# Twelve rounded layer-0 steps with their lower halves on GpSimd, six of sixteen chunks scaled in PSUM

## Chip, cores and metric

The kernel runs on one core of a Trainium2 chip. The metric is the device time of one execution in microseconds (us), as the median of several runs. The engines are called TensorE (PE in the rows; PEld is its weight load), VectorE (DVE), ScalarE (ACT), GpSimd (POOL) and SyncE (SP, which only issues transfers here).

## What is computed

The input has 512 rows of 64 fields with 16 elements each. Three layers follow; each makes the products of all fields of its input with the 64 original fields, and mixes them with a weight matrix into 128 outputs. Each layer's output is summed over the 16 elements and the three sums are put side by side.

```python
x_vec = input
outs = []
for W, b in params:
    z = jnp.einsum('bhd,bfd->bhfd', x_vec, input)
    B, h, f, d = z.shape
    z = z.reshape(B, h * f, d)
    x_vec = jnp.einsum('oc,bcd->bod', W, z) + b[None, :, None]
    outs.append(x_vec.sum(axis=2))
return jnp.concatenate(outs, axis=1)
```

Shapes: `input` is 512x64x16, `W0` is 128x4096, `W1` and `W2` are 128x8192, the result is 512x384, all float32.

## The kernel before

**Tiling.** A tile is 8 input rows times 16 elements, 128 columns. Four tiles make a group of 512 columns, and there are 16 groups. `body(n, kind)` exists once on each engine and runs for group 0 ("first"), groups 1 to 14 ("inner") and group 15 ("last"). Within it the place `e` runs from 0 to 63: tile `j = e // 16`, chunk `c = e % 16`. All engines walk the same places, each in its own written order, and wait for one another by semaphores.

**Layer 1, the bulk.** At each place `chunk` (L1008) makes y = x1 times 512 columns of W1 in three matmuls (`by_parts`, L875). Weights and x1 are split into an upper part, rounded to float32r, and a lower part, the rest; the products are upper by upper, upper by lower, lower by upper. A chunk covers four fields, and its 128x512 result lies in one of four PSUM banks (`y0` to `y3`, bank `c % 4`). The result must be multiplied by the four fields of x0 (`x0t`, one scalar per partition and field) and added up over all fields. It goes one of three ways:

- direct (`add_fields`, L716): VectorE multiplies and adds the bank into `acc` with four instructions of 128x128 (L738, L740);
- scaled (`SCALED`): ScalarE multiplies the bank in place with four instructions (`scale`, L627), then VectorE adds all 512 columns to `acc` with one instruction (L725);
- helped (`HELPED`): ScalarE writes the products to `prod` in SBUF (`multiply`, L638), and GpSimd adds them to `pacc` (`add_products`, L443 and L445).

Of 16 chunks, five are helped (1, 4, 7, 10, 13), three scaled (3, 9, 15) and eight direct. `chunk` waits until the chunk four before it, which had the same bank, has been taken out. Around an add, VectorE waits for its own instructions: L725 waits until the direct chunk before it is finished, and the first direct instruction behind L725 waits until L725 is finished (`acc_step`).

GpSimd's `combine` (L447) adds `acc` and `pacc` of the tile before (L451), folds the four fields (L453, L456) and so makes `x2`, which `layer2` (L996) needs at chunk 12 of the following tile. `own_rows` (L690) makes the other operand of `layer2` on VectorE, once a tile.

**Layer 0, one group ahead.** Layer 0 of group n+1 is made during group n in 17 steps, at the places `AHEAD_AT` (9, 11, 14, 17, 20, 23, 26, 29, 32, 34, 37, 40, 43, 46, 49, 52, 55; in group 0 between 24 and 55, and group 0's own steps at places 3 to 13 with 384 columns). For each step SyncE brings a shifted copy of the fields into one of six slots of `z`, and GpSimd multiplies it by the fields (`product`, L435). A step in `WHOLE` is one float32 matmul (L901). A step in `PARTED` (1, 3, 5, 7, 9, 11, 13) is three float32r matmuls: ScalarE first rounds `z` to `zh` (`part_upper`, L503, six places ahead), and VectorE subtracts to get `zl` (`part_lower`, L679, four places ahead). Step 16 is a small rest (`left_parts`, `left_lower` at L687). A slot of `z` is given back to SyncE when `zl` is made, or for a whole step when TensorE has used it (`slot_free`, L342).

**Turn of the group.** At place 58 VectorE makes the lower part of three tiles of the next group's x1 (`lower`, L706, 128x384), at place 4 that of the last tile (128x128), and at place 6 it sums layer 0 (L713). In groups 4, 8 and 12 the third layer's matmuls for a quarter of the rows (L992) are put between places 18 and 25.

## Time and profile before

| | |
|---|---|
| median of 3 runs | 1110.55 us (1109.91 to 1111.24) |
| the profiled execution's own time | 1111.36 us |
| its span | 1109.6 us |
| granted TensorE clock, mean over the span | 0.991 |
| busy: TensorE, VectorE, ScalarE, GpSimd | 1078.9, 863.8, 713.5, 862.1 us |
| L740 on VectorE (direct) | 1792 instructions, 493.2 us busy |
| L725 on VectorE (adds of scaled chunks) | 192 instructions, 132.6 us busy |
| L679 on VectorE (lower parts) | 112 instructions, 104.8 us busy |
| L696 on VectorE (`own_rows`) | 64 instructions, 41.6 us busy |
| L445 and L443 on GpSimd (adding products) | 256 instructions, 343.3 us busy |
| L503 on ScalarE (rounding) | 112 instructions, 70.4 us busy |

The span runs from the first to the last instruction. Busy time of an engine is the union of its instructions; a TensorE matmul's end is modelled, since matmuls overlap, so the pace of TensorE is better read from the starts of like matmuls in the timeline. Idle time in a row is the time in which that engine had nothing running just before the instruction, with the releaser.

### The profile page before, as it was taken

The page shows a single profiled execution, that of the slowest core. Times are in us where ns is not written, and L with a number is a line of the kernel's source. Part 1 is how long each engine was busy: PE and PEld are TensorE (multiplying, and loading weights), DVE is VectorE, ACT ScalarE, POOL GpSimd, SP SyncE. Part 2 cuts the span into 40 slices and gives each one's busy share as a digit, 9 for nine tenths or more (in the row PEclk, how much of TensorE's full clock was granted, in tenths as well). Part 3 has the DMA queues.
Part 4 walks back from the last instruction along what each step waited for, and adds up shares of the span by engine and source line. Part 5 has one row for each costly group of instructions (what it writes and reads, how often), then busy time and mean ns, then how long its engine had stood idle before and what let it go on. Part 6 is the DMA issues. An engine that isn't in the chain of part 4 may idle for free.

```text
span 1109.6 us, 17740 instructions
## 1 busy us (share of the span) xinstructions
PE 1078.9 (97%) x4781; PEld 808.4 (73%) x4781; DVE 863.8 (78%) x2529; ACT 713.5 (64%) x2428; POOL 862.1 (78%) x727
## 2 busy tenths in 40 slices
PE   6889999999999999999999999999999999999997
PEld 5767677777778777777778777777777877777776
DVE  5665888889894788988885698888887588888981
ACT  2566767767673676767673676766766476676771
POOL 2457897989984799897976779797988579798560
PEclk8999999999999999999999999999999999999998
DMA  7743333223241332324332142333232232321000
GB/s 280 196 101 96 74 92 79 77 55 96 50 101 39 66 84 54 97 65 86 84 67 58 45 87 82 70 93 74 77 68 64 63 69 77 79 77 41 1 23 8
DMA packets 108325, 85.87 MB, mean 77 GB/s; under 512 B 71040, under 2 KB 73824, under 8 KB 108096
## 3 DMA queue, kind: packets, MB, share of 16 engines
q1 hardware_dynamic: 106832, 78.17, 28.5%
q10 hardware_dynamic: 1392, 6.55, 1.9%
q8 instruction: 38, 0.62, 0.2%
q14 instruction: 63, 0.52, 0.2%
HBM read 14.75 MB, written 0.79 MB: 14 GB/s over the span
## 4 chain that ended last, share of the span: by engine, by line
PE 85%; DVE 6%; ACT 5%; issue 2%; DMA 1%; POOL 1%; ACTq 0%; DVEq 0%
PE y L881 57%; PE l L901 11%; PE l L881 7%; PE xt L992 5%; PE l2p L1004 3%; DVE acc L740 3%; ACT prod L638 2%; ACT y L627 2%; DVE acc L725 1%; DMA gram<-in_L_rec_W_dram 1%; DVE gram L824 1%; PE l L951 1%; PE l2p L981 1%; ACT x1h L536 1%; DVE bd L696 0%
## 5 line engine op out<-in xcount | busy, mean ns | idle before, releaser
L740 DVE SCALAR_TENSOR_TENSOR acc<-y,x0t,acc 128x128 f32<-128x128 f32 x1792 | 493.2, 340 | 62.6 <-PE y L881 58.2
L638 ACT ACTIVATE prod<-y,x0t 128x128 f32<-128x128 f32 x1280 | 367.7, 380 | 221.7 <-PE y L881 215.3
L881 PE MATMUL y<-w1h,x1h 128*128 128x512 f32 x1024 | 469.1, 458 | 3.9 <-DVE acc L740 3.7
L881 PE MATMUL y<-w1h,x1l 128*128 128x512 f32 x1024 | 402.7, 393 | 0.0
L881 PE MATMUL y<-w1l,x1h 128*128 128x512 f32 x1024 | 401.8, 392 | 0.0
L435 POOL TENSOR_TENSOR z<-z,xg 128x512 f32<-128x512 f32 (+2 forms) x272 | 372.2, 1373 | 24.4 <-DMA z<-xg 24.4
L445 POOL TENSOR_TENSOR pacc<-pacc,prod 128x512 f32<-128x512 f32 x192 | 253.1, 1318 | 137.2 <-ACT prod L638 137.2
L881 PEld LDWEIGHTS y<-w1h,x1h 128*128 128x128 f32 x1024 | 193.5, 189 | 108.4 <-issue 40.6
L627 ACT ACTIVATE y<-y,x0t 128x128 f32<-128x128 f32 x768 | 215.2, 349 | 75.8 <-PE y L881 75.5
L881 PEld LDWEIGHTS y<-w1l,x1h 128*128 128x128 f32 x1024 | 193.2, 189 | 59.5 <-issue 29.0
L725 DVE TENSOR_TENSOR acc<-y,acc 128x512 f32<-128x512 f32 x192 | 132.6, 691 | 131.8 <-ACT y L627 129.6
L881 PEld LDWEIGHTS y<-w1h,x1l 128*128 128x128 f32 x1024 | 192.5, 188 | 42.9
L901 PE MATMUL l<-z,w0t 128*128 128x512 f32 (+1 forms) x288 | 144.8, 584 | 0.0
L443 POOL TENSOR_TENSOR pacc<-prod 128x512 f32<-128x512 f32 x64 | 90.2, 1410 | 43.9 <-ACT prod L638 43.9
L679 DVE TENSOR_TENSOR zl<-z,zh 128x512 fp32r<-128x512 f32 (+1 forms) x112 | 104.8, 935 | 0.8 <-ACT zh L503 0.8
L503 ACT CAST zh<-z 128x512 fp32r<-128x512 f32 (+1 forms) x112 | 70.4, 629 | 40.7 <-POOL z L435 40.3
L451 POOL TENSOR_TENSOR pacc<-pacc,acc 128x512 f32<-128x512 f32 x63 | 81.2, 1289 | 6.1 <-DVE acc L725 4.6
L992 PEld LDWEIGHTS xt<-gram,w2t 128*128 128x128 f32 x512 | 63.8, 199 | 3.2 <-ACT sums L543 1.2
L992 PE MATMUL xt<-gram,w2t 128*128 128x128 f32 x512 | 64.1, 283 | 0.8 <-ACT sums L543 0.8
L901 PEld LDWEIGHTS l<-z,w0t 128*128 128x128 f32 x288 | 53.8, 188 | 11.2
L738 DVE TENSOR_SCALAR acc<-y,x0t 128x128 f32<-128x128 f32 x192 | 54.9, 341 | 0.0
L453 POOL TENSOR_TENSOR pacc<-pacc 128x256 f32<-128x256 f32 x63 | 46.7, 742 | 4.9
(92 smaller groups left out, 652.6 us busy)
## 6 DMA issues: line engine op xcount, KB each, us to landing
z<-xg SPq DMA_DIRECT2D x480, 128.0 KB, 2.4
w2t<-in_L_rec_W_dram SPq DMA_DIRECT2D x8, 512.0 KB, 9.0
gram<-in_L_rec_W_dram ACTq DMA_DIRECT2D x8, 512.0 KB, 4.7
xg<-in_r_input_dram SPq DMA_DIRECT2D x30, 128.0 KB, 3.9
z<-xg SPq DMA_DIRECT2D x32, 96.0 KB, 2.7
z<-xg SPq DMA_DIRECT2D x15, 192.0 KB
gram<-in_L_rec_W_dram ACTq DMA_DIRECT2D x1, 2048.0 KB, 9.7
out_dram<-z SPq DMA_DIRECT2D x4, 192.0 KB, 1.9
```

The costliest lines, as they stand in the source:

```text
L435: nc.gpsimd.tensor_tensor(to[0:rows, :], to[0:rows, :], xg[0:rows, cols], ALU.mult).then_inc(z_made, 1)
L443: nc.gpsimd.tensor_tensor(pacc[:], prod[:, 0], prod[:, 1], ALU.add).then_inc(pool_step, 1)
L445: nc.gpsimd.tensor_tensor(pacc[:], pacc[:], prod[:, h % HSLOTS], ALU.add).then_inc(pool_step, 1)
L451: nc.gpsimd.tensor_tensor(pacc[:], pacc[:], acc[:, slot], ALU.add).then_inc(pool_step, 1)
L627: last = nc.scalar.activation(of, of, ACT.Copy, scale=x0t[:, j, f:f + 1])
L638: last = nc.scalar.activation(prod[:, h % HSLOTS, k, :], y[c % YB][:, k * O:(k + 1) * O], ACT.Copy, scale=x0t[:, j, f:f + 1])
L679: nc.vector.tensor_tensor(zl[:, i % ZHSLOTS, cols], zin(n, t), zh[:, i % ZHSLOTS, cols].bitcast(F32), ALU.subtract).then_inc(zl_made, 1)
L725: nc.vector.tensor_tensor(to, y[c % YB][:], to, ALU.add).then_inc(acc_step, 1)
L740: ins = nc.vector.scalar_tensor_tensor(out=to, in0=of, scalar=x0t[:, j, f:f + 1], in1=b1r[:] if m == 0 else to, op0=ALU.mult, op1=ALU.add)
L881: ins = nc.tensor.matmul(to, stationary, moving, start=(first and k == 0), stop=(last and k == 2))
L901: nc.tensor.matmul(l0[:, cols], w0t[:, WHOLE.index(t), :], zin(n, t), start=(t == 0), stop=False).then_inc(z_used, 1)
L992: last = nc.tensor.matmul(l2, w2t[:, f, :], gram[:, f, :], start=(f == 0), stop=(f == F - 1))
```

## The change

`PARTED` becomes all steps of the first 16 that aren't divisible by four: twelve rounded steps instead of seven, four whole instead of nine. `part_lower` moves from VectorE to GpSimd and gets three slots of `zl`; `zh` has three slots, shared with the rest step. `HELPED` shrinks to chunks 7 and 13, so that GpSimd adds once a tile; `SCALED` grows to 1, 3, 5, 9, 11, 15 (1, 3, 5, 9, 11, 12 in the last group); the eight others stay direct. `multiply` now waits for the whole of the tile before (`x2_made`), since `pacc` is gone and the sum is made in `prod`. `own_rows` moves to ScalarE as four instructions of 128x64. GpSimd's order is written by places: products eight places ahead (the first three of the group after next at 59, 61 and 63), lower parts four ahead, the combination of the tile before at chunk 4, the add at chunk 15.

```diff
-PARTED = tuple(range(1, 15, 2))
+PARTED = tuple(t for t in range(ZT - 1) if t % 4)
...
-ZHSLOTS = 2
+ROUNDED = PARTED + (ZT - 1,)
+RN = len(ROUNDED)
+ZHSLOTS = 3
+ZLSLOTS = 3
...
-HELPED = (1, 4, 7, 10, 13)
+HELPED = (7, 13)
 HN = len(HELPED)
 SUMMED = tuple(c for c in range(CHUNKS) if c not in HELPED)
-SCALED = (3, 9, 15)
-SCALED_LAST = (3, 9, 12)
+SCALED = (1, 3, 5, 9, 11, 15)
...
-HSLOTS = 3
...
 PARTED_AT = [{AHEAD_AT[t] - k: t for t in PARTED} for k in (6, 4)]
...
-PRODUCTS_AT = ((2, 1, 1, 1, 1), (1, 1, 1, 1, 1), (1, 1, 1, 1, 1), (1, 0, 0, 0, 0))
...
+PRODUCTS_AT = [AHEAD_AT[t] - 8 for t in range(ZT)]
+PRODUCTS_EARLY_AT = (59, 61, 63)
+ADD_AT = [c + 2 for c in HELPED]
+COMBINE_AT = 4
...
-        prod = sb("prod", [P, HSLOTS, CF, O])
-        pacc = sb("pacc", [P, CF, O])
+        prod = sb("prod", [P, HN, CF, O])
...
-                if h == 1:
-                    pool.wait_ge(x2_made, x2_ready(tile - 1))
-                    nc.gpsimd.tensor_tensor(pacc[:], prod[:, 0], prod[:, 1], ALU.add).then_inc(pool_step, 1)
-                else:
-                    nc.gpsimd.tensor_tensor(pacc[:], pacc[:], prod[:, h % HSLOTS], ALU.add).then_inc(pool_step, 1)
+                nc.gpsimd.tensor_tensor(prod[:, 0], prod[:, 0], prod[:, h], ALU.add).then_inc(pool_step, 1)
+
+            def part_lower(n, t):
+
+                i = PN * n + PARTED.index(t)
+                cols = LATER if n == 0 else slice(0, GROUP)
+                if i >= ZLSLOTS:
+                    before = i - ZLSLOTS
+                    pool.wait_ge(z_used, ZT * (before // PN) + PARTED[before % PN] + 1)
+                pool.wait_ge(zh_made, i + 1)
+                nc.gpsimd.tensor_tensor(zl[:, i % ZLSLOTS, cols], zin(n, t),
+                                        zh[:, zhslot(n, t), cols].bitcast(F32), ALU.subtract).then_inc(zl_made, 1)
...
+                part = prod[:, 0]
+                pool.wait_ge(prod_made, HN * tile + 2 * HN)
                 pool.wait_ge(acc_step, tile_added(tile))
                 pool.wait_ge(pool_step, pool_at(tile, HN - 1))
-                nc.gpsimd.tensor_tensor(pacc[:], pacc[:], acc[:, slot], ALU.add).then_inc(pool_step, 1)
...
+                        for t in range(ZT):
+                            if at[t] == e and (kind == "first" or t >= len(PRODUCTS_EARLY_AT)):
+                                product(n + 1, t)
+                        if e in lower_at[1]:
+                            part_lower(n + 1, lower_at[1][e])
+                    if c == COMBINE_AT and (kind != "first" or j > 0):
                         combine(tile - 1, (j - 1) % 2)
...
+                        if c == ADD_AT[h]:
+                            add_products(tile, h)
+                    if e in PRODUCTS_EARLY_AT and n + 2 < GROUPS:
+                        product(n + 2, PRODUCTS_EARLY_AT.index(e))
...
+            def slot_of_parts(n, t):
+
+                i = rounded(n, t)
+                if i >= ZHSLOTS:
+                    before = i - ZHSLOTS
+                    act.wait_ge(z_used, ZT * (before // RN) + ROUNDED[before % RN] + 1)
+                return i % ZHSLOTS
...
+                    if c == OWN_AT:
+                        own_rows(tile, j)
...
+            def own_rows(tile, j):
+
+                act.wait_ge(l2p_made, layer2_ready(tile - 2))
+                act.wait_ge(own_made, 1)
+                for b in range(HALF_B):
+                    last = nc.scalar.activation(bd[:, j % 2, b * F:(b + 1) * F], x0t[:, j, :], ACT.Copy,
+                                                scale=own_half[:, b:b + 1])
+                last.then_inc(bd_made, 1)
...
-                before = h - HSLOTS if h >= HSLOTS else max(range(h, HN, HSLOTS))
-                act.wait_ge(pool_step, pool_at(tile, max(before, 1) - (POOL_STEPS if h < HSLOTS else 0)))
+                act.wait_ge(x2_made, x2_ready(tile - 1))
...
-            def part_lower(n, t):
-
-                i = PN * n + PARTED.index(t)
-                cols = LATER if n == 0 else slice(0, GROUP)
-                dve.wait_ge(zh_made, i + 1)
-                nc.vector.tensor_tensor(zl[:, i % ZHSLOTS, cols], zin(n, t),
-                                        zh[:, i % ZHSLOTS, cols].bitcast(F32), ALU.subtract).then_inc(zl_made, 1)
...
-            def own_rows(tile, j):
-
-
-                dve.wait_ge(l2p_made, layer2_ready(tile - 2))
-                dve.wait_ge(own_made, 1)
-                shape = [P, HALF_B, F]
-                nc.vector.tensor_tensor(bd[:, j % 2, 0:GRAM].rearrange("p (b f) -> p b f", f=F),
-                                        x0t[:, j, :].unsqueeze(1).to_broadcast(shape),
-                                        own_half[:].unsqueeze(2).to_broadcast(shape), ALU.mult).then_inc(bd_made, 1)
...
-                    if c == OWN_AT:
-                        own_rows(n * TILES + j, j)
...
-                    if kind == "inner" and e in PARTED_AT[1]:
-                        part_lower(n + 1, PARTED_AT[1][e])
...
                     i = PARTED.index(t)
-                    at = (PN * n + i) % ZHSLOTS
                     pe.wait_ge(zl_made, PN * n + i + 1)
-                    by_parts(l0[:, cols], zh[:, at, cols], zl[:, at, cols], w0h[:, i, :], w0l[:, i, :],
-                             t == 0, False, False).then_inc(z_used, 1)
+                    by_parts(l0[:, cols], zh[:, zhslot(n, t), cols], zl[:, (PN * n + i) % ZLSLOTS, cols],
+                             w0h[:, i, :], w0l[:, i, :], t == 0, False, False).then_inc(z_used, 1)
```

On VectorE the order changes at every tile. The first rows are from an inner group, tile 0 from its first chunk (`y0`, b1r) to the add of chunk 9, before:

```order
L740 SCALAR_TENSOR_TENSOR acc<-y0,x0t,b1r 128x128
L738 TENSOR_SCALAR acc<-y0,x0t 128x128 x3
L740 SCALAR_TENSOR_TENSOR acc<-y2,x0t,acc 128x128 x4
L725 TENSOR_TENSOR acc<-y3,acc 128x512
L706 SCALAR_TENSOR_TENSOR x1l<-l0,b0c,x1h 128x128
L740 SCALAR_TENSOR_TENSOR acc<-y1,x0t,acc 128x128 x4
L713 TENSOR_REDUCE sums<-l0 128x32
L740 SCALAR_TENSOR_TENSOR acc<-y2,x0t,acc 128x128 x4
L679 TENSOR_TENSOR zl<-z,zh 128x512
L740 SCALAR_TENSOR_TENSOR acc<-y0,x0t,acc 128x128 x4
L725 TENSOR_TENSOR acc<-y1,acc 128x512
```

and the same stretch of the changed kernel, up to the add of chunk 9:

```order
L763 SCALAR_TENSOR_TENSOR acc<-y0,x0t,b1r 128x128
L761 TENSOR_SCALAR acc<-y0,x0t 128x128 x3
L748 TENSOR_TENSOR acc<-y1,acc 128x512
L763 SCALAR_TENSOR_TENSOR acc<-y2,x0t,acc 128x128 x4
L748 TENSOR_TENSOR acc<-y3,acc 128x512
L729 SCALAR_TENSOR_TENSOR x1l<-l0,b0c,x1h 128x128
L763 SCALAR_TENSOR_TENSOR acc<-y0,x0t,acc 128x128 x4
L748 TENSOR_TENSOR acc<-y1,acc 128x512
L736 TENSOR_REDUCE sums<-l0 128x32
L763 SCALAR_TENSOR_TENSOR acc<-y2,x0t,acc 128x128 x4
L763 SCALAR_TENSOR_TENSOR acc<-y0,x0t,acc 128x128 x4
L748 TENSOR_TENSOR acc<-y1,acc 128x512
```

The one L679 that stood here is gone, and where one L725 stood at chunk 3, there are now three, at chunks 1, 3 and 5, each between two direct chunks.

On GpSimd an inner group's stretch between two combinations (that of tile 0 and that of tile 1) reads before, with `pacc<-pacc,acc` the start of the second combination:

```order
L435 TENSOR_TENSOR z<-z,xg 128x512
L443 TENSOR_TENSOR pacc<-prod 128x512
L435 TENSOR_TENSOR z<-z,xg 128x512
L445 TENSOR_TENSOR pacc<-pacc,prod 128x512
L435 TENSOR_TENSOR z<-z,xg 128x512
L445 TENSOR_TENSOR pacc<-pacc,prod 128x512
L435 TENSOR_TENSOR z<-z,xg 128x512
L445 TENSOR_TENSOR pacc<-pacc,prod 128x512
L435 TENSOR_TENSOR z<-z,xg 128x512
L451 TENSOR_TENSOR pacc<-pacc,acc 128x512
```

and in the changed kernel, from the product at place 21 to the start of the second combination:

```order
L448 TENSOR_TENSOR z<-z,xg 128x512
L464 TENSOR_TENSOR zl<-z,zh 128x512
L448 TENSOR_TENSOR z<-z,xg 128x512
L464 TENSOR_TENSOR zl<-z,zh 128x512
L448 TENSOR_TENSOR z<-z,xg 128x512 x2
L464 TENSOR_TENSOR zl<-z,zh 128x512
L454 TENSOR_TENSOR prod<-prod 128x512
L448 TENSOR_TENSOR z<-z,xg 128x512
L464 TENSOR_TENSOR zl<-z,zh 128x512
L448 TENSOR_TENSOR z<-z,xg 128x512
L464 TENSOR_TENSOR zl<-z,zh 128x512
L473 TENSOR_TENSOR prod<-prod,acc 128x512
```

Three of four adds of products are gone from a tile, and lower parts (`zl`) stand between the products instead.

## Rows read from the trace of the kernel before

**Rows 1.** The profile's page, span and busy time of each engine

```profile
span 1109.6 us, 17740 instructions
...
PE 1078.9 (97%) x4781; PEld 808.4 (73%) x4781; DVE 863.8 (78%) x2529; ACT 713.5 (64%) x2428; POOL 862.1 (78%) x727
```

**Rows 2.** Windows: span, then busy us (records) of each engine

```profile
513.10:527.80 14.70, 14.66 (x59) 10.43 (x60) 13.94 (x41) 11.11 (x40) 14.54 (x13) 1.00 0.22 58
560.10:574.40 14.30, 14.12 (x59) 10.12 (x58) 11.37 (x36) 10.34 (x37) 8.87 (x9) 1.00 0.54 106
513.10:574.40 61.30, 61.08 (x252) 44.66 (x253) 52.44 (x156) 42.96 (x150) 54.61 (x46) 1.00 0.32 77
1032.50:1083.20 50.70, 49.68 (x217) 37.02 (x217) 46.12 (x146) 39.65 (x145) 30.25 (x28) 1.00 0.04 13
```

**Rows 3.** Timeline of TensorE, two layer-0 steps: start us, length us, instruction

```profile
587.21 0.39 PE L881 MATMUL y<-w1l,x1h 128*128 128x512 f32 x1
...
587.66 1.02 PE L901 MATMUL l<-z,w0t 128*128 128x512 f32 x2
...
588.75 0.39 PE L881 MATMUL y<-w1l,x1h 128*128 128x512 f32 x1
...
590.14 0.39 PE L881 MATMUL y<-w1l,x1h 128*128 128x512 f32 x1
...
591.51 0.39 PE L881 MATMUL y<-w1l,x1h 128*128 128x512 f32 x1
```

**Rows 4.** Timeline of TensorE, tile 3 chunk 8 to the next tile 0 chunk 10

```profile
567.96 0.40 PE L881 MATMUL y<-w1l,x1h 128*128 128x512 f32 x1
...
573.60 0.39 PE L881 MATMUL y<-w1l,x1h 128*128 128x512 f32 x1
...
574.41 0.47 PE L881 MATMUL y<-w1h,x1h 128*128 128x512 f32 x1 [0.19 <-DVE acc L740]
574.72 0.39 PE L881 MATMUL y<-w1l,x1h 128*128 128x512 f32 x1
...
582.72 0.39 PE L881 MATMUL y<-w1l,x1h 128*128 128x512 f32 x1
```

**Rows 5.** Timeline of VectorE: chunks 8 to 11; the end of a tile

```profile
522.17 1.11 DVE L740 SCALAR_TENSOR_TENSOR acc<-y,x0t,acc 128x128 f32<-128x128 f32 x4
523.39 0.69 DVE L725 TENSOR_TENSOR acc<-y,acc 128x512 f32<-128x512 f32 x1
524.18 1.12 DVE L740 SCALAR_TENSOR_TENSOR acc<-y,x0t,acc 128x128 f32<-128x128 f32 x4
...
575.60 0.69 DVE L725 TENSOR_TENSOR acc<-y,acc 128x512 f32<-128x512 f32 x1 [0.31 <-ACT y L627]
576.21 0.34 DVE L740 SCALAR_TENSOR_TENSOR acc<-y,x0t,b1r 128x128 f32<-128x128 f32 x1
```

**Rows 6.** Timeline of ScalarE, one chunk scaled in PSUM

```profile
528.12 1.11 ACT L627 ACTIVATE y<-y,x0t 128x128 f32<-128x128 f32 x4 [0.56 <-PE y L881]
```

**Rows 7.** Groups by line and shape: count, busy us, mean ns, idle

```profile
L679 DVE TENSOR_TENSOR zl<-z,zh 128x512 fp32r<-128x512 f32 x105 | 100.4, 956 | 0.8 <-ACT zh L503 0.8
...
L453 POOL TENSOR_TENSOR pacc<-pacc 128x256 f32<-128x256 f32 x63 | 46.7, 742 | 4.9
...
L456 POOL TENSOR_TENSOR x<-pacc 128x128 f32<-128x128 f32 x63 | 32.5, 516 | 4.9
...
L713 DVE TENSOR_REDUCE sums<-l 128x32 f32<-128x512 f32 x16 | 10.9, 680 | 0.0
L687 DVE TENSOR_TENSOR zleft<-z,zleft 32x512 fp32r<-32x512 f32 x15 | 10.3, 687 | 0.5
L706 DVE SCALAR_TENSOR_TENSOR x1l<-l,b0c,x1h 128x384 fp32r<-128x384 f32 x16 | 9.7, 607 | 0.0
...
L951 PE MATMUL l<-acc,w0t 128*128 128x128 f32 x6 | 1.0, 275 | 0.0
```

**Rows 8.** GpSimd line L435: shortest, median, longest ns

```profile
L435 POOL TENSOR_TENSOR z<-z,xg x272: 991/1291/1775, 22.4 to 1019.0; 128x512 f32<-128x512 f32 x120, 128x384 f32<-128x384 f32 x8, 96x512 f32<-96x512 f32 x7, 96x384 f32<-96x384 f32 x1
```

89 lines of the change are left out of this document (42 added, 47 removed).

## Prediction

> **What bounds the kernel now.** I read the page first: TensorE is busy for 1078.9 of 1109.6 us, VectorE and GpSimd for 78% each [rows 1]. An average hides which stretch has which limit, so I went to the windows of one inner group. Its 61.3 us are 14.7 in tile 0, 14.3 in tile 3 and so 32.3 in tiles 1 and 2; VectorE is busy for 52.4 us of the group, but for 13.94 of 14.70 in tile 0 [rows 2]. The reason is the schedule: no layer-0 step stands between places 56 and 8, so TensorE turns out chunks fastest just there. Then the timelines. The second matmul of a chunk starts at 588.75 and that of the chunk two later at 590.14, so a chunk alone costs 0.695 us; with a whole step between, the distance is 1.54, with a rounded one 1.37 [rows 3]. A whole step therefore costs 0.85 and a rounded one 0.68. The last of the views shows the first sign of the other limit: the last chunk of tile 3 comes 1.12 us behind its forerunner instead of 0.695, because VectorE (releaser L740) had not emptied the bank [rows 4]. TensorE is the bound, with VectorE close behind at the turn of the group.
>
> **What the rounded steps give.** Five steps a group go from 0.85 to 0.68: -0.85 us in each of the 15 groups made ahead, of which bodies 1 to 14 are the inner ones.
>
> **What VectorE loses and gets.** In each inner group it loses seven lower parts (0.96 us each in the mean [rows 7]) and four `own_rows`. It gets three more adds a tile, twelve a group. Their price is in the timeline [rows 5]. Four direct instructions take 1.11 us and each lasts 0.34, so they start 0.26 apart: 1.04 a chunk. The add starts 0.11 behind the end of the fourth (522.17 + 1.11 = 523.28, then 523.39), lasts 0.69, and the next chunk starts 0.10 behind its end (524.08, then 524.18). From the fourth direct instruction's start (522.94) to the next chunk's first it is 1.24 instead of 0.26: **an add between two direct chunks costs 0.98**, not 0.69. At a tile's end nothing waits behind the add (575.60 to 576.21 is 0.61), so it costs 0.11 + 0.08 + 0.61 = 0.80.
>
> A tile of VectorE before: 8 x 1.04 + 2 x 0.98 + 0.80 = 11.1. After, with five adds inside and one at the end: 8.3 + 4.9 + 0.8 = **14.0**. TensorE's chunks of a tile, without steps, take 16 x 0.695 = 11.1. In tiles 1 and 2 five or six steps a tile keep TensorE slower than VectorE. In tiles 3 and 0 they don't.
>
> **The turn of the group.** Take the stretch from the start of tile 3's chunk 8 to that of the next tile 0's chunk 10. Today it takes 14.76 (567.96 to 582.72), 0.43 of it the wait above [rows 4]; none of its steps changes its form. In the changed order it begins when VectorE has emptied chunk 4's bank and ends when it has emptied that of tile 0's chunk 6. Between these lie nine direct chunks (6, 8, 10, 12, 14, 0, 2, 4, 6), six adds inside (5, 9, 11, 1, 3, 5) and one at the tile's end (15): 9.36 + 5.88 + 0.80. Add the lower parts of x1 (0.607 less the overlap of 0.08, so 0.52; and 0.26 for the narrow one) and the sum (0.60) [rows 7]. These three fill the waits beside an add, 0.18 each, so -0.54. It makes 16.9, **+2.1 us** against 14.76.
>
> Before the stretch VectorE is late already. From the start of tile 2's last chunk TensorE needs nine chunks and the steps 14, 15 and 16 (0.68, 0.68, about 0.24) to reach chunk 8: 7.9. On the other side: the chunk (0.7), 0.2 to ScalarE, scaling 1.11 [rows 6], then on VectorE the add 0.61, chunk 0 1.04, add 0.98, chunk 2 1.04, add 0.80, the rest step's subtraction (0.687 [rows 7] and a gap, 0.72), chunk 4 1.12, and 0.2 to TensorE: 8.5. That is +0.6 to +0.8. About 0.2 more is a wait in tile 1, which VectorE enters three chunks behind. Sum of an inner group: -0.85 + 2.1 + 0.75 + 0.2 = **+2.2**, in 14 groups +31 us. A group then takes 63.5, though VectorE's work in it is only 4 x 14.0 + 2.1 = 58.
>
> **Last group.** No steps slow TensorE, so VectorE sets the pace throughout. With chunks 11 and 12 both scaled, a tile is 8.3 + 4 x 0.98 + 1.77 (two adds in a row: 0.19 + 0.69 + 0.10 + 0.69 + 0.10) = 14.0; four tiles, x1 and sum: 56.5 against 50.7 now [rows 2]. **+5.8.**
>
> **First group and start.** Five more steps have two weights instead of one in the early layer-0 matmuls: three of those (six records, two a float32 matmul) took 1.0 us [rows 7], so five take up to 1.7, on the path to the first chunk; from below, nothing, if something else is late there. I take +1.3. In group 0 the steps are 384 columns wide (5 x 0.13 saved) and tile 3 begins to suffer; GpSimd no longer stands waiting for products of chunks there. I take 0, with -2 and +4 as ends.
>
> **ScalarE.** Five more roundings, four x four `own_rows` instructions of 64 columns. These shapes aren't in the trace; from below, nothing, from above the 0.26 pace of 128 columns [rows 6], 1.04 a tile. With 5 x 0.55 that is at most 6.9 us on 43.0 busy of 61.3 [rows 2]: 49.9 of 63.5, hidden in its waits for TensorE. If the cover went, as much as 0.3 a tile in the last group: +1.
>
> **GpSimd.** Twelve adds of products go, twelve lower parts come. Its products of the same shape take 1.29 in the median, 1.775 at the longest [rows 8]; the lower part on GpSimd isn't in the trace. Between 0.99 and 1.775 I take 1.29, the nearest row: same shape, same kind, two inputs in SBUF. From the lower part of step 5 to that of step 14 it must issue 9 products, 7 lower parts, one add and two combinations (1.29 + 0.74 + 0.52 each [rows 7, 8]): 17 x 1.29 + 5.1 = 27.0 us, while TensorE walks the places 19 to 45 in 26 chunks, 3 whole and 6 rounded steps, 18.1 + 2.6 + 4.1 = 24.8, besides two layer-2 products and the transposes. So GpSimd works there almost without a pause, up to 2 us behind, against the four places (2.8 us and their steps) that a lower part is ahead: just covered. Behind a late lower part TensorE itself stands, behind a late combination ScalarE at chunk 7. SyncE gets twelve slots back from GpSimd; its transfers are issued in the same order, and a late early product at 59 holds up an add that is needed only at chunk 12 of the next tile.
>
> **Sum.** 31 + 5.8 + 1.3 + 0 = +38. Against the profiled execution's 1111.4 this is 1149.5; the median of the runs is 0.8 below that execution, so I predict **1148.5 us**.
>
> **Rivals.** *The waits around an add cost nothing* (4%). Then an add costs 0.61, the turn takes 9.36 + 7 x 0.61 + 1.38 = 15.0 and so +0.25, without the late entry: -0.6 a group, -8 in all; the last group is back at its 50 us; with the start 1103. For it: nothing in the rows; against it: both gaps are there at each such add [rows 5]. The Trainium skill says in "VectorE: DVE Perf Modes", section "The DRAIN you can't avoid", that the semaphore costs nothing extra. By that rule the time is this rival's; the trace disagrees, with instructions 0.26 apart where no wait is and 0.10 behind the end where one is.
>
> *GpSimd becomes the bound* (14%). If a lower part takes 1.6 instead of 1.29, the seven of the middle cost 2.2 more, some 1.7 of it behind its cover: +24, 1172 us. It decides from about 1.4. For it: products of up to 1.775; against it: the median of 1.29. The Trainium skill's "SBUF — State Buffer", section "Who interferes with whom", says that a VectorE instruction with two SBUF inputs contends with GpSimd's reads. By that rule the long products came from lower parts and `own_rows`, which go, and this rival loses weight; no row here shows GpSimd without them for a whole group.
>
> *TensorE stays the bound* (4%), with the four banks swallowing VectorE's lateness: only the rounded steps count, -13 - 0.6 + 1.3, 1098 us. Against it: the 0.43 lost today with three adds a tile fewer.
>
> *It cancels* (2%): gain and loss within 0.2%, which is about what a measurement of this kernel can tell from no change.
>
> **Numbers.** The forecast has 76%. Its own ends are a loss of 1.6 to 2.9 a group (22 to 41) with the rest as above: 1139 to 1162. Reaching into the GpSimd case the range is 1138 to 1170 and leaves out under 2 in 10. Faster 0.08, same 0.02, slower 0.90.
>
> **What would show it.** Right: tiles 3 and 0 of an inner group together at 31 to 32 (29.0 now), tiles 1 and 2 at about 32 as now; the bank waits of TensorE on L725's and L740's successors from place 56 to 10; VectorE with gaps of 0.1 around each add and hardly any other idle time there; the last group at 56.5. Wrong: GpSimd without idle time and TensorE waiting for `zl`; adds closer than 0.1 to their neighbours; tiles 3 and 0 unchanged.

## The result and the profile after

The changed kernel takes 1155.43 us in the median of four runs (1153.61 to 1156.08), the kernel before, run beside it, 1110.89 (1109.91 to 1112.77): ratio 1.0393, interval 1.0378 to 1.0409. It is 44.5 us slower. The profiled execution took 1155.74 us.

The page, span and busy time of each engine, which answers to [rows 1]:

```profile
span 1154.0 us, 18359 instructions
...
PE 1092.7 (95%) x4871; PEld 810.9 (70%) x4871; DVE 884.8 (77%) x2545; ACT 817.7 (71%) x2759; POOL 813.2 (70%) x727
```

TensorE's share has fallen from 97% to 95%, and VectorE's busy time has grown by only 21 us. Busy time doesn't show where 44 us went. The windows do: tile 0, tile 3 and the whole of the same inner group as in [rows 2], and the last group.

```profile
533.04:548.84 15.80, 15.20 (x61) 10.19 (x60) 14.22 (x43) 12.14 (x44) 12.49 (x12) 1.00 0.24 61
581.42:596.90 15.48, 14.30 (x60) 10.17 (x59) 13.42 (x39) 11.79 (x44) 8.29 (x9) 1.00 0.58 119
533.04:596.90 63.86, 61.87 (x258) 44.55 (x257) 53.51 (x158) 49.58 (x171) 51.17 (x46) 1.00 0.31 74
1070.52:1127.87 57.35, 53.35 (x217) 35.37 (x215) 52.44 (x154) 43.36 (x159) 14.56 (x17) 1.00 0.03 11
```

Tiles 3 and 0 take 31.3 us together (29.0 before), tiles 1 and 2 the rest, 32.6 here and 32.25 in most groups. The starts of the first chunk of each group in the two traces share the loss out: before the first chunk +1.7, group 0 +4.6 (98.0 to 102.65), the 14 inner groups +31.35 (901.7 to 933.1, which is 2.24 each), the last group +6.6 (50.8 to 57.35), the tail +0.1.

TensorE's timeline over the turn of the group, from tile 3 chunk 8 to tile 0 chunk 10, against [rows 4]:

```profile
589.39 0.40 PE L895 MATMUL y<-w1l,x1h 128*128 128x512 f32 x1
...
591.09 0.50 PE L895 MATMUL y<-w1h,x1h 128*128 128x512 f32 x1 [0.28 <-DVE acc L763]
...
596.59 0.47 PE L895 MATMUL y<-w1h,x1h 128*128 128x512 f32 x1 [0.25 <-DVE acc L763]
...
601.55 0.50 PE L895 MATMUL y<-w1h,x1h 128*128 128x512 f32 x1 [0.27 <-DVE acc L763]
...
603.64 0.50 PE L895 MATMUL y<-w1h,x1h 128*128 128x512 f32 x1 [0.32 <-DVE acc L763]
...
606.40 0.39 PE L895 MATMUL y<-w1l,x1h 128*128 128x512 f32 x1
```

The stretch takes 606.40 - 589.39 = 17.01 us; it was 14.76. Where one wait of 0.19 stood, TensorE now stops again and again, each time until VectorE (releaser L763) has emptied a bank. VectorE's timeline over chunks 4 to 9 of tile 3 and at its end, against [rows 5], shows what it does meanwhile:

```profile
587.88 1.13 DVE L763 SCALAR_TENSOR_TENSOR acc<-y,x0t,acc 128x128 f32<-128x128 f32 x4
589.11 0.69 DVE L748 TENSOR_TENSOR acc<-y,acc 128x512 f32<-128x512 f32 x1
589.91 2.16 DVE L763 SCALAR_TENSOR_TENSOR acc<-y,x0t,acc 128x128 f32<-128x128 f32 x8
592.17 0.69 DVE L748 TENSOR_TENSOR acc<-y,acc 128x512 f32<-128x512 f32 x1
...
597.74 0.69 DVE L748 TENSOR_TENSOR acc<-y,acc 128x512 f32<-128x512 f32 x1 [0.26 <-ACT y L669]
598.35 0.34 DVE L763 SCALAR_TENSOR_TENSOR acc<-y,x0t,b1r 128x128 f32<-128x128 f32 x1
```

The add comes 589.11 - 589.01 = 0.10 behind the fourth direct instruction and the next chunk 589.91 - 589.80 = 0.11 behind the add, for every add with direct chunks on both sides. At the tile's end VectorE has a longer pause: before the add of chunk 15 it waits 0.26 us for ScalarE. In tile 0 of the last group VectorE also has an instruction that no other group has:

```profile
1078.59 0.48 DVE L786 TENSOR_SCALAR sums<-sums,b0d 128x512 f32<-128x512 f32 x1
```

Two prices had no row before: the own rows, in ScalarE's timeline, and the lower part on GpSimd, of whose lines L464 (lower parts) and L448 (products) the shortest, median and longest duration (ns) follow:

```profile
591.86 1.07 ACT L659 ACTIVATE bd<-x0t,own_half 128x64 f32<-128x64 f32 x4
```

```profile
L464 POOL TENSOR_TENSOR zl<-z,zh x192: 991/1287/1310, 38.3 to 1056.5; 128x512 fp32r<-128x512 f32 x180, 128x384 fp32r<-128x384 f32 x12
...
L448 POOL TENSOR_TENSOR z<-z,xg x272: 991/1292/1325, 23.1 to 1054.0; 128x512 f32<-128x512 f32 x120, 128x384 f32<-128x384 f32 x8, 96x512 f32<-96x512 f32 x7, 96x384 f32<-96x384 f32 x1
```

A lower part takes GpSimd 1.287 us in the median (VectorE took 0.956 in the mean), the same as a product, whose longest has fallen from 1.775 to 1.325 [rows 8]. Last, a row of TensorE's waits in group 0 (total us, times, longest), where it had waited for VectorE's `zl` before (2.6 us in three waits):

```profile
PE l L895 <- POOL zl L464: 6.6, 3, 5.3
```

### The profile page after: what moved, and what is told of

Read it like the earlier page. It is cut to its first block, busy times and chain, and to the rows that moved or that the text cites. A ratio compares the mean times of both kernels' runs of the same rounds, so it can differ in the third digit from the quotient of the medians.

```text
span 1154.0 us, 18359 instructions
## 1 busy us (share of the span) xinstructions
PE 1092.7 (95%) x4871; PEld 810.9 (70%) x4871; DVE 884.8 (77%) x2545; ACT 817.7 (71%) x2759; POOL 813.2 (70%) x727
## 4 chain that ended last, share of the span: by engine, by line
PE 61%; DVE 20%; ACT 9%; issue 5%; POOL 2%; DMA 2%; DVEq 0%; ACTq 0%; SPq 0%; POOLq 0%
PE y L895 38%; DVE acc L763 11%; PE l L895 8%; DVE acc L748 6%; PE xt L1005 5%; PE l L914 4%; ACT y L669 4%; PE l2p L1017 3%; ACT prod L679 3%; DVE acc L761 2%; ACT gram L572 1%; DMA gram<-in_L_rec_W_dram 1%; POOL z L448 1%; POOL zl L464 1%; ACT zh L535 1%
## 5 line engine op out<-in xcount | busy, mean ns | idle before, releaser
L763 DVE SCALAR_TENSOR_TENSOR acc<-y,x0t,acc 128x128 f32<-128x128 f32 x1792 | 496.2, 344 | 68.3 <-PE y L895 40.7
L669 ACT ACTIVATE y<-y,x0t 128x128 f32<-128x128 f32 x1536 | 428.8, 347 | 160.3 <-PE y L895 158.8
L448 POOL TENSOR_TENSOR z<-z,xg 128x512 f32<-128x512 f32 (+2 forms) x272 | 344.3, 1272 | 70.2 <-DMA z<-xg 70.1
L748 DVE TENSOR_TENSOR acc<-y,acc 128x512 f32<-128x512 f32 x384 | 265.6, 692 | 144.5 <-ACT y L669 119.5
L464 POOL TENSOR_TENSOR zl<-z,zh 128x512 fp32r<-128x512 f32 (+1 forms) x192 | 243.6, 1270 | 120.1 <-ACT zh L535 119.8
L679 ACT ACTIVATE prod<-y,x0t 128x128 f32<-128x128 f32 x512 | 146.1, 369 | 99.5 <-PE y L895 66.1
L454 POOL TENSOR_TENSOR prod<-prod 128x512 f32<-128x512 f32 x64 | 82.3, 1287 | 111.6 <-ACT prod L679 111.6
L473 POOL TENSOR_TENSOR prod<-prod,acc 128x512 f32<-128x512 f32 x63 | 81.4, 1292 | 3.0 <-DVE acc L763 1.9
L895 PE MATMUL l<-zh,w0h 128*128 128x512 f32 (+1 forms) x192 | 76.8, 400 | 6.6 <-POOL zl L464 6.6
L895 PE MATMUL l<-zl,w0h 128*128 128x512 f32 (+1 forms) x192 | 74.9, 390 | 0.0
L895 PE MATMUL l<-zh,w0l 128*128 128x512 f32 (+1 forms) x192 | 74.8, 390 | 0.0
L1005 PEld LDWEIGHTS xt<-gram,w2t 128*128 128x128 f32 x512 | 63.6, 199 | 3.4 <-ACT sums L574 1.3
L1005 PE MATMUL xt<-gram,w2t 128*128 128x128 f32 x512 | 63.9, 282 | 0.7 <-ACT sums L574 0.7
L914 PE MATMUL l<-z,w0t 128*128 128x512 f32 (+1 forms) x128 | 64.5, 585 | 0.0
```

The source lines that it names most:

```text
L448: nc.gpsimd.tensor_tensor(to[0:rows, :], to[0:rows, :], xg[0:rows, cols], ALU.mult).then_inc(z_made, 1)
L454: nc.gpsimd.tensor_tensor(prod[:, 0], prod[:, 0], prod[:, h], ALU.add).then_inc(pool_step, 1)
L464: nc.gpsimd.tensor_tensor(zl[:, i % ZLSLOTS, cols], zin(n, t), zh[:, zhslot(n, t), cols].bitcast(F32), ALU.subtract).then_inc(zl_made, 1)
L473: nc.gpsimd.tensor_tensor(part, part, acc[:, slot], ALU.add).then_inc(pool_step, 1)
L669: last = nc.scalar.activation(of, of, ACT.Copy, scale=x0t[:, j, f:f + 1])
L679: last = nc.scalar.activation(prod[:, h, k, :], y[c % YB][:, k * O:(k + 1) * O], ACT.Copy, scale=x0t[:, j, f:f + 1])
```

## The experiments

Two causes were to be told apart. **VectorE**: the gaps beside an add make VectorE the bound at the turn of the group and in the last one. **GpSimd**: its lower parts or combinations come late, and VectorE's waits only follow. Twelve kernels ran, each timed beside the kernel before (1111.7 to 1112.4 us). Ratios are against that; times of groups are distances between first chunks in the profiled executions.

### Half of each lower part, and another order in group 0

The first kernel makes half of the columns of each lower part; the other half stays zero, so these columns of layer 0 lack their lower part.

```diff
+            nc.gpsimd.memset(zl[:].rearrange("p s n -> p (s n)").bitcast(F32), 0.0)
...
-                nc.gpsimd.tensor_tensor(zl[:, i % ZLSLOTS, cols], zin(n, t),
-                                        zh[:, zhslot(n, t), cols].bitcast(F32), ALU.subtract).then_inc(zl_made, 1)
+                of = zin(n, t)
+                w = (cols.stop - cols.start) // 2
+                some = slice(cols.start, cols.start + w)
+                nc.gpsimd.tensor_tensor(zl[:, i % ZLSLOTS, some], of[:, 0:w],
+                                        zh[:, zhslot(n, t), some].bitcast(F32), ALU.subtract).then_inc(zl_made, 1)
```

> The changed kernel, but GpSimd makes only the first half of the columns of every lower part; the other columns of zl are left at what was written into them once at the start. That takes about 0.5 us from each of twelve GpSimd operations of a group and nothing from another engine. VectorE theory: inner groups stay at 63.6 within 0.2 and the last group at 57.4, only the first group may gain 1 to 3 us; in all 1151 to 1156. GpSimd theory: the inner groups go back towards 60.5, in all 1105 to 1125.

Measured: 1153.01 us (1.0365, 1.0346 to 1.0384). Inner groups stay at 63.6, the last at 57.35; group 0 falls from 102.65 to 100.6. The other kernel leaves the work as it is and changes GpSimd's order in group 0 alone:

```diff
-LATER_PRODUCTS_AT = [LATER_AT[t] - 4 for t in range(ZT)]
+LATER_PRODUCTS_AT = [LATER_AT[t] - (4 if t < LSLOTS else 3) for t in range(ZT)]
...
                     if kind == "first":
-                        for t in range(ZT):
-                            if LATER_PRODUCTS_AT[t] == e:
-                                product(0, t)
                         for t in PARTED:
                             if LATER_PARTED_AT[1][t] == e:
                                 part_lower(0, t)
+                        for t in range(ZT):
+                            if LATER_PRODUCTS_AT[t] == e:
+                                product(0, t)
```

> The changed kernel, but in group 0 GpSimd's lower parts stand ahead of the products of the same place, and the products of steps 8 to 16, whose slots must first come free and be filled again, stand one place later. Theory of the first group: in the changed kernel GpSimd waits 3.7 and 1.7 us for transfers of steps 8 and 9 while the lower parts of steps 5 and 6, ready to be made, stand behind them, and TensorE waits 5.3 us for those; with the order changed tile 0 of group 0 goes from 39.7 to 35 to 36.5 us, all else stays, in all 1151 to 1152.5. Rival (the lower parts wait for ScalarE's roundings, not for the transfers): tile 0 stays at 39 to 40, in all 1155.

Measured: 1150.36 us (1.0345, 1.0329 to 1.0360), 5.1 less than the changed kernel, and group 0 is 96.2 us, all other groups unchanged. GpSimd's timeline in the changed kernel shows what was mended:

```profile
40.28 2.01 POOL L464 TENSOR_TENSOR zl<-z,zh 128x384 fp32r<-128x384 f32 x2
45.94 1.00 POOL L448 TENSOR_TENSOR z<-z,xg 128x384 f32<-128x384 f32 x1 [3.65 <-DMA z<-xg]
48.62 1.94 POOL L448 TENSOR_TENSOR z<-z,xg 128x384 f32<-128x384 f32 x2 [1.69 <-DMA z<-xg]
50.52 1.95 POOL L464 TENSOR_TENSOR zl<-z,zh 128x384 fp32r<-128x384 f32 x2
```

GpSimd waits 3.65 and 1.69 us for transfers whose products stand ahead, in its order, of two lower parts that could be made at once. TensorE waits 5.3 us for these. The same stretch with the lower parts first:

```profile
41.77 2.00 POOL L464 TENSOR_TENSOR zl<-z,zh 128x384 fp32r<-128x384 f32 x2
43.70 1.05 POOL L448 TENSOR_TENSOR z<-z,xg 128x384 f32<-128x384 f32 x1
44.68 2.04 POOL L464 TENSOR_TENSOR zl<-z,zh 128x384 fp32r<-128x384 f32 x2
46.70 1.01 POOL L448 TENSOR_TENSOR z<-z,xg 128x384 f32<-128x384 f32 x1
48.38 1.03 POOL L448 TENSOR_TENSOR z<-z,xg 128x384 f32<-128x384 f32 x1 [0.67 <-DMA z<-xg]
```

So the loss of group 0 is GpSimd's order (6.4 us there) more than its load (2.0), and has nothing to do with the inner groups, where halving the load changes nothing.

### The scaled chunks in a sum of their own

Direct chunks go on adding into one sum; scaled ones go into a second, which ScalarE begins with the product of chunk 1, so that neither waits for the other. GpSimd then takes in the second sum in place of a product. Two things change along with it: chunk 1 is helped instead of chunk 7, and its product, which has a buffer for each of two tiles in turn, no longer waits for the tile before.

```diff
-HELPED = (7, 13)
+HELPED = (1, 13)
...
-SCALED = (1, 3, 5, 9, 11, 15)
...
+SCALED = (3, 5, 7, 9, 11, 15)
...
+                pool.wait_ge(acc_step, added(tile, scaled_in(tile)[-1]))
...
-                nc.gpsimd.tensor_tensor(prod[:, 0], prod[:, 0], prod[:, h], ALU.add).then_inc(pool_step, 1)
+                nc.gpsimd.tensor_tensor(prod[:, 0], prod[:, 0], prod[:, 1 + tile % 2], ALU.add).then_inc(pool_step, 1)
...
                     if c == COMBINE_AT and (kind != "first" or j > 0):
+                        add_products(tile - 1, 1)
                         combine(tile - 1, (j - 1) % 2)
-                    for h in range(1, HN):
-                        if c == ADD_AT[h]:
-                            add_products(tile, h)
...
-                act.wait_ge(x2_made, x2_ready(tile - 1))
+                act.wait_ge(x2_made, x2_ready(tile - (1 if h else 2)))
...
-                    to = acc[:, j % 2].rearrange("p k o -> p (k o)")
...
+                    to = prod[:, 1 + tile % 2].rearrange("p k o -> p (k o)")
```

> The changed kernel, but the scaled chunks are added into a second sum (a buffer that ScalarE starts with chunk 1's products), so that an add never follows or precedes an instruction on the same sum; helped chunks are 1 and 13, scaled 3, 5, 7, 9, 11, 15. The same number of adds, direct chunks, roundings and GpSimd operations as in the changed kernel; only what an add waits for is taken away. VectorE theory (an add between two direct chunks costs 0.98 us because of the two waits, and the turn of the group is paced by that): an add then costs 0.61, a tile 12.0 us of VectorE instead of 14.0, an inner group 60.0 to 60.6 instead of 63.6, the last group 50 to 51 instead of 57.4; in all 1155 - 46 - 7 = 1102 us, between 1097 and 1108. GpSimd theory (the twelve lower halves hold the group up): the group stays at 63.6, in all 1148 to 1155. Theory of mere work (VectorE has too many adds, whatever they wait for): an add costs 0.69, less than 1 us a group is won, 1140 to 1150.

Measured: 1153.33 us (1.0371, 1.0354 to 1.0388), not 1102. But only the total looks like the GpSimd theory's. The last group fell from 57.35 to 53.5, and tiles 0 and 3 from 15.8 and 15.5 to 14.95 and 15.05; tile 1 grew from 15.9 to 17.25 and tile 2 from 16.35 to 16.8, which took it all back. Windows of tile 1 (columns as in [rows 2]):

```profile
548.82:566.06 17.24, 15.91 (x71) 12.19 (x70) 11.99 (x37) 12.57 (x43) 14.39 (x14) 1.00 0.25 68
```

GpSimd's timeline in that tile, and TensorE's wait there:

```profile
551.94 1.28 POOL L465 TENSOR_TENSOR zl<-z,zh 128x512 fp32r<-128x512 f32 x1 [2.53 <-DVE acc L766]
553.19 1.29 POOL L455 TENSOR_TENSOR prod<-prod 128x512 f32<-128x512 f32 x1
554.64 1.30 POOL L474 TENSOR_TENSOR prod<-prod,acc 128x512 f32<-128x512 f32 x1 [0.17 <-DVE acc L766]
...
558.51 1.26 POOL L465 TENSOR_TENSOR zl<-z,zh 128x512 fp32r<-128x512 f32 x1
```

```profile
559.83 0.50 PE L898 MATMUL l<-zh,w0h 128*128 128x512 f32 x1 [1.33 <-POOL zl L465]
```

The add of the second sum (L455) now stands at chunk 4, right in front of the combination, and the lower part of place 26 behind both is 1.3 us late. The edit had removed one wait and made another: chunk 15, the last scaled one, kept GpSimd from adding earlier.

The next kernel puts just this right: chunk 15 goes into the main sum again, and GpSimd adds the second sum at chunk 15 of its own tile. A further one has the mended order of group 0 as well.

```diff
+                    if c == scaled_in(tile)[-1]:
+                        dve.wait_ge(acc_step, added(tile, SUMMED[m - 1]))
+                        to = acc[:, j % 2].rearrange("p k o -> p (k o)")
...
-                pool.wait_ge(acc_step, added(tile, scaled_in(tile)[-1]))
+                pool.wait_ge(acc_step, added(tile, scaled_in(tile)[-2]))
...
-                        add_products(tile - 1, 1)
...
+                    for h in range(1, HN):
+                        if c == ADD_AT[h]:
+                            add_products(tile, h)
```

> Like the kernel with a second sum, but the scaled chunk of place 15 goes into the main sum again, so that GpSimd can take in the second sum at chunk 15 of its own tile, as the changed kernel does, and not at chunk 4 of the next. If GpSimd's late add was what lengthened tile 1 (17.25 against 15.9 us) and tile 2 there, these two go back to 15.9 and 16.35 to 16.5, tiles 3 and 0 stay at about 15.0 each: an inner group takes 62.2 to 62.6 us, the last group 53.5 to 54.0, the first about 103, the whole 1130 to 1137 us. If the long tile 1 came from VectorE or ScalarE (their own order is nearly the same as in the kernel with a second sum), tile 1 stays above 17 and the whole at about 1153.

> The same as two_sums_early, with the mended order of GpSimd in group 0 (lower parts ahead of products, products of steps 8 and later one place later). The two gains lie in different groups and should add: first group 96 to 97 us, the others as in two_sums_early, the whole 1123 to 1131 us. It would beat the kernel before (1111) only if inner groups fell below 61.3 us, which TensorE's own work in tiles 1 and 2 (32.2 us there) does not allow with tiles 3 and 0 above 14.5 each.

Measured: 1122.31 us (1.0096, 1.0078 to 1.0113), better than expected, and 1116.05 (1.0038, 1.0024 to 1.0052). Inner groups take 61.6 us, the last 53.6, group 0 103.3 and 95.65. The windows of tile 0, tile 3, the inner group and the last group of the first of the two:

```profile
521.40:536.35 14.95, 14.75 (x62) 10.44 (x60) 13.57 (x43) 12.28 (x45) 12.79 (x12) 1.00 0.25 64
568.39:582.99 14.60, 14.42 (x61) 10.23 (x60) 13.04 (x41) 11.62 (x43) 9.07 (x9) 1.00 0.61 126
521.40:582.99 61.59, 61.21 (x259) 45.10 (x258) 51.18 (x158) 49.34 (x171) 51.72 (x46) 1.00 0.32 77
1042.62:1096.23 53.61, 52.07 (x217) 36.05 (x215) 49.88 (x154) 43.68 (x161) 14.90 (x17) 1.00 0.03 12
```

Its VectorE timeline, two adds with a direct chunk ahead of each:

```profile
575.40 0.68 DVE L758 TENSOR_TENSOR prod<-y,prod 128x512 f32<-128x512 f32 x1
576.00 1.11 DVE L774 SCALAR_TENSOR_TENSOR acc<-y,x0t,acc 128x128 f32<-128x128 f32 x4
577.03 0.68 DVE L758 TENSOR_TENSOR prod<-y,prod 128x512 f32<-128x512 f32 x1
577.63 1.12 DVE L774 SCALAR_TENSOR_TENSOR acc<-y,x0t,acc 128x128 f32<-128x128 f32 x4
```

Same instructions, same shapes: a direct chunk and an add now take 577.63 - 576.00 = 1.63 us, where the changed kernel took 589.91 - 587.88 = 2.03. An add costs 0.60 (577.63 - 577.03) without the two waits and 0.98 with them. The kernel is 33.1 us faster than the changed one. Of the 31.6 us between the two profiled executions 28.1 lie in the inner groups, 2.0 in each, and 3.7 in the last. The other things that the edit changes have no share in it that the trace shows: ScalarE's products of chunk 7 did wait for the tile before in the changed kernel, but none of TensorE's waits there was for them.

### One chunk back to GpSimd, and the own rows back to VectorE

If VectorE is the bound, less work for it must help; if GpSimd is just covered, an add more for it must hurt.

```diff
-HELPED = (7, 13)
+HELPED = (7, 11, 13)
...
-SCALED = (1, 3, 5, 9, 11, 15)
-SCALED_LAST = (1, 3, 5, 9, 11, 12)
+SCALED = (1, 3, 5, 9, 15)
+SCALED_LAST = (1, 3, 5, 9, 12)
...
```

> The changed kernel with chunk 11 helped instead of scaled: one add a tile less on VectorE (0.98 us between two direct chunks), one add of products a tile more on GpSimd (1.29 us, 5.2 us a group). VectorE theory: tile 3 and the last group get shorter by about 1 us a tile; an inner group 63.6 - 1.0 = 62.6, the last group 57.4 - 4 = 53.5; in all 1155 - 14 - 4 = 1137 us, between 1130 and 1143. GpSimd theory: GpSimd has 5.2 us more to do in a group, tiles 1 and 2 get longer, in all 1165 to 1220.

Measured: 1173.51 us (1.0555, 1.0539 to 1.0570). Tile 0, tile 2 and the inner group:

```profile
541.29:557.64 16.35, 15.60 (x61) 10.11 (x60) 13.38 (x41) 12.59 (x46) 13.35 (x13) 1.00 0.24 63
573.52:590.97 17.45, 16.74 (x70) 12.06 (x68) 12.71 (x39) 12.93 (x44) 16.68 (x15) 1.00 0.15 43
541.29:606.51 65.22, 62.57 (x258) 44.59 (x257) 51.39 (x153) 49.62 (x170) 56.48 (x50) 1.00 0.30 73
```

VectorE has 2.1 us a group less to do, and the inner groups are 1.5 us longer in the median: GpSimd works for 16.68 of tile 2's 17.45 us and is the bound there. It was just covered, with less than one add a tile to spare. Why tile 0 grew too was not followed up. Tile 3, which the VectorE theory had about 1 us shorter, stays at 15.55: the next tile's first chunk comes 0.5 us earlier behind its forerunner, but the step at place 52 has 0.7 us more to wait, for GpSimd's lower part.

The last group has no lower parts, and GpSimd is busy for 20.3 us of it, so a gain can't be hidden by its load there. VectorE's busy time falls by 3.0 us in it, to 49.4, and yet it takes 57.8 us (57.35 in the changed kernel), where the VectorE theory had 53.5. VectorE has no add at chunk 11 now, and stands idle before that of chunk 12 until ScalarE has scaled it. Its timeline in tile 1 of the last group:

```profile
1116.38 0.69 DVE L748 TENSOR_TENSOR acc<-y,acc 128x512 f32<-128x512 f32 x1 [0.93 <-ACT y L669]
```

In that tile the chunks from 4 to 10, where adds stand between direct chunks, come as far apart as before. So an add's price counts where TensorE waits behind it; the sum of VectorE's work over a tile doesn't set the pace of the last group, and at chunk 12 ScalarE is as late as VectorE was.

The own rows on VectorE again, one instruction a tile at chunk 11:

```diff
-                for b in range(HALF_B):
-                    last = nc.scalar.activation(bd[:, j % 2, b * F:(b + 1) * F], x0t[:, j, :], ACT.Copy,
-                                                scale=own_half[:, b:b + 1])
...
+                nc.vector.tensor_tensor(bd[:, j % 2, 0:GRAM].rearrange("p (b f) -> p b f", f=F),
+                                        x0t[:, j, :].unsqueeze(1).to_broadcast(shape),
+                                        own_half[:].unsqueeze(2).to_broadcast(shape), ALU.mult).then_inc(bd_made, 1)
```

> The changed kernel with the own rows made by VectorE again (one instruction a tile at chunk 11, as in the kernel before), so ScalarE loses four instructions a tile. If ScalarE is late in the last group because of them (it measured +6.6 us where VectorE's count gave +5.8), the last group gains up to 0.8, against up to 0.7 a tile that VectorE gets: last group 56.5 to 60. In inner groups chunk 11 of tiles 1 and 2 has time to spare; in tiles 0 and 3 VectorE gets 0.6 to 0.9 us more, so the group takes 63.7 to 65.3 us: the whole 1156 to 1178. If ScalarE and not VectorE set the pace of tiles 3 and 0, the group gets shorter than 63.6 instead.

Measured: 1158.03 us (1.0415, 1.0398 to 1.0433); inner groups take 63.9 (63.7 in the changed kernel), the last 57.6 (57.35). Tiles 3 and 0 got shorter by 0.4 us together and tile 2 longer by 0.5. So moving `own_rows` back doesn't pay. That they cost nothing on ScalarE isn't shown, since they went from one engine to the other. In the last group four more instructions on VectorE make only 0.3 us, which again says that its sum of work isn't the bound there.

### Fewer rounded steps, and steps at other places

```diff
-PARTED = tuple(t for t in range(ZT - 1) if t % 4)
+PARTED = tuple(range(1, 15, 2))
...
```

> The changed kernel with its old seven rounded steps (odd steps 1 to 13) beside the left-over step; all else as in the changed kernel, so GpSimd makes seven lower parts a group instead of twelve. By the step prices (0.85 whole, 0.68 rounded) five steps cost 0.85 us more a group where TensorE sets the pace (the steps 6 and 10 in tiles 1 and 2 for certain, 0.34 us) and less where VectorE does (2, 14 and 15 in tiles 0 and 3): inner groups 63.9 to 64.5 us, start 1.3 to 1.7 us earlier, first group 0 to 6 us shorter since GpSimd has less to do there: the whole 1150 to 1165. If GpSimd's load were the bound of the changed kernel, the inner groups would get shorter than 63 and the whole fall below 1140.

Measured: 1162.12 us (1.0453, 1.0434 to 1.0472). Inner groups take 64.0 (63.7 with twelve), 0.3 more in the median and 0.5 in the mean, since one of them takes 65.3. So five rounded steps give 0.3 to 0.5 of the 0.85. The chunk distances show where the rest goes: each of the five steps is 0.16 to 0.19 shorter with rounding, but behind the two in tile 3 the distance to its chunk 8, which waits for VectorE, is 1.85 instead of 1.38. Five lower parts less bring GpSimd nothing that TensorE feels, and in group 0 TensorE still waits for it (103.7 us).

```diff
-AHEAD_AT = [9 + t * 46 // (ZT - 1) for t in range(ZT)]
+AHEAD_AT = [9 + 3 * t for t in range(ZT)]
```

> The changed kernel with the seventeen layer-0 steps three places apart, at places 9 to 57 and not 9 to 55, so that tile 2 has five steps and tile 3 three and the left-over one; nothing else. If TensorE sets the pace of tile 2 (16.35 us) and VectorE that of tiles 3 and 0, the step that moves takes 0.68 us out of tile 2 and costs less than that in tile 3: inner groups 62.9 to 63.4 us instead of 63.6, the whole 1144 to 1152. If TensorE sets the pace in tiles 3 and 0 too, moving a step changes nothing: 63.5 to 63.9 and 1154 to 1157 us. A loss is possible if x1 comes late for the next tile 0 (it has two places less): up to 1 us a group.

> The kernel before with the steps three places apart. There TensorE sets the pace in all four tiles but for 0.4 to 0.5 us at the turn of the group, so a step that moves from tile 2 to tile 3 (0.68 us) should change nothing: inner groups 61.1 to 61.5 us, the whole within 3 us of the kernel before. If tiles 3 and 0 had room there (VectorE late in them), it gains up to 0.5 us a group, 7 us.

> The second sum with GpSimd's add at chunk 15, the mended order of group 0, and the steps three places apart. From 61.6 us an inner group loses up to 0.68 in tile 2 and gets back 0 to 0.5 in tile 3, where VectorE is now just behind TensorE: 60.9 to 61.4 us, the whole 1106 to 1114 us against 1112 for the kernel before, so between 0.5% faster and 0.2% slower. If x1 is late it stays at 1116.

Measured: 1149.85 us (1.0349, 1.0328 to 1.0370) in the changed kernel, whose inner groups fall to 63.1: tiles 1 and 2 lose 0.3 and 0.45, tile 3 gets 0.35 longer. The same edit makes the kernel before 3.5 us slower (1115.15; 1.0030, 1.0016 to 1.0043; inner groups 61.5), just over the 3 expected at most, and the one with two sums 6.6 slower than without it, against the expected gain (1122.63; 1.0107, 1.0087 to 1.0127; inner groups 61.9, with tile 3 at 15.3 for 14.6). A step moved into tile 3 costs half of its 0.68 where TensorE waits for VectorE there, and all of it where not; why the two-sums kernel lost rather than stayed the same was not settled.

### A version to beat both

Against the kernel with two sums and the mended order:

```diff
-HELPED = (1, 13)
+HELPED = (3, 7)
...
-SCALED = (3, 5, 7, 9, 11, 15)
-SCALED_LAST = (3, 5, 7, 9, 11, 12)
+SCALED = (5, 9, 11, 13, 15)
+SCALED_LAST = (5, 9, 11, 12, 13)
...
```

> The second sum with the mended order of group 0, and other chunks for each engine: ScalarE multiplies 3 and 7 for GpSimd (into two buffers a tile in turn, so that it never waits for the tile before), scales 5, 9, 11, 13 and 15, and VectorE takes 1 and the even ones directly, nine chunks a tile and five adds. In the kernel with eight direct ones what is left of TensorE's waits stands at the chunks 3, 7, 9 and 11, four behind a scaled one: 0.2 us to ScalarE, 1.12 of scaling and 0.69 of the add come to just over the three chunks (2.04 us) that the other banks last. If that chain is the cause, the waits at 7 and 11 go, an inner group falls from 61.6 to 60.9 to 61.3 us, the last from 53.6 to 52.0 to 53.0, the whole from 1116 to 1104 to 1111 us against 1112 for the kernel before. If VectorE's load is the cause (nine direct chunks take 0.4 us a tile more), inner groups take 61.8 to 62.8 and the last 54 to 55: 1119 to 1133 us.

Measured: 1120.93 us (1.0088, 1.0072 to 1.0105). In inner groups the waits at chunks 7 and 11 went, but for a part of that at chunk 7 of tile 3, as the chain through ScalarE had it, and others came at chunks 1 to 5 of tile 0 (15.5 us for 14.95); the group takes 61.5 (61.6 before the edit), between what the two theories had. The last group went back to 57.6, more than either had: the three scaled chunks 11 to 13 keep ScalarE busy there for 3.18 us on end, and VectorE waits 0.25, 0.34 and 0.34 us for them, one by one. No version beat the kernel before; the nearest, with two sums and the mended order, is 0.38% behind it.

## Why the prediction was right

The forecast was 1148.5 us in 1138 to 1170, slower by way of VectorE's adds, and 1155.43 came. Point by point:

- **An add between two direct chunks costs 0.98.** Right: 0.10, 0.69 and 0.11 in the trace after, as read from [rows 5], and the experiment that takes the two waits away brings an add to 0.60 and the kernel 33 us down. One reading beside it is wrong, without harm to the sum: the chunk that came 1.12 us behind its forerunner in [rows 4] is the first of tile 0, at 574.72, not the last of tile 3.
- **The turn of the group, +2.1.** 16.9 us forecast, 17.01 measured.
- **The inner group, +2.2, 14 of them +31.** 2.24 measured, +31.35. The parts came out too, within 0.2: in the median of the inner groups the distance to tile 3's chunk 8 grew from 0.93 to 1.85, where the lateness had been put at 0.6 to 0.8, and that behind tile 1's chunk 9 from 0.68 to 0.93. But they aren't independent. The -0.85 of "five steps a group go from 0.85 to 0.68" brings 0.3 to 0.5 against the kernel with seven rounded steps, since what is saved in tile 3 comes back as lateness at its chunk 8.
- **Last group, +5.8.** +6.6. "Four tiles of 14.0, x1 and sum" is what was mis-sized: the tiles take 14.95, 14.08, 14.39 and 13.93, so 0.95 more in tile 0 and 0.4 in tile 2 where I had 0.5 in all. In tile 0 the count left out VectorE's L786, 0.48 us long. That the other tiles come so near 14.0 is in part luck, for "VectorE sets the pace throughout" isn't borne out: with one add a tile less the count gives 13.0, but tiles 1 and 2 stay at 14.0 and 14.4 and the group at 57.8. The "+1 if the cover of ScalarE goes" isn't it as written: `own_rows` costs ScalarE 1.07 us a tile, as bounded, and moving it back gains nothing; but whether ScalarE's lateness at chunk 12 has a share in the +6.6 stays open.
- **First group, "I take 0".** This is the largest miss, +4.6, above its own upper end of +4. The step that failed is "GpSimd no longer stands waiting for products of chunks there": it stands waiting for transfers instead, and the lower parts are queued behind that wait. The text had asked who is queued behind a waiting GpSimd only for the inner groups.
- **Start, +1.3.** +1.7, but not a measurement: see the last section.
- **GpSimd just covered, at 1.29 a lower part.** 1.287, and in inner groups TensorE waits for `zl` hardly at all; half of each lower part left out gains nothing there, one add more a tile loses 18 us. The rival in which GpSimd becomes the bound needed 1.4. The Trainium skill's "SBUF — State Buffer", section "Who interferes with whom", says that a VectorE instruction with two SBUF inputs contends with GpSimd's reads; the longest product fell from 1.775 to 1.325 when VectorE's lower parts and `own_rows` went, and that agrees, as does the kernel in which `own_rows` came back to VectorE, with 1.511.
- **The rival in which the waits cost nothing** fell in both ways. They cost 33 us; and without them the time isn't 1103 but 1116 with group 0 mended, and the last group stays 2.8 above before. Five adds at 0.60 and the one at chunk 15 are still work, and a scaled bank still passes through two engines; how the rest divides between these two isn't shown. The Trainium skill's "VectorE: DVE Perf Modes", section "The DRAIN you can't avoid", says of eight copies in a row that the semaphore costs nothing extra. If that held for these instructions, the two kernels with the same adds would take the same; they differ by 0.38 an add.
- **TensorE stays the bound**, and **it cancels**: the banks did not swallow it; the waits at the turn say so.
- **The forecast's own ends** were added up unevenly: 22 to 41 for the inner groups in place of 31 gives 1139.5 to 1158.5, and only with the +4 of the first group is the upper end 1162. The time measured lies within either.

Of the 44.5 us, then: 33 go with the waits around the adds, 6 with GpSimd's order in group 0, and the other 5 are what the second-sum kernel with the mended order still has over the kernel before (4 over the kernel before as timed beside it). In the traces that is the heavier last group (+2.8), 0.24 in each inner group (+3.4) and a later start (+2.3), less what group 0 has gained (-2.4).
